# Window attention with a routed feed-forward: the score product in two 64x64 tiles instead of four 32x32, with some TensorE and VectorE work moved behind the product

## What is computed

```
xs = roll(layernorm_c(x)) for a shift of 0 and of 2        # along channels and rows
for each half of the channels (32) and each shift:
    q, k, v = split(qkv_w @ xs)                            # 1x1 convolution, 8 heads of 4 channels
    lepe = depthwise 3x3 convolution of v
    in each window of 4 x 4 pixels, for each head:
        out = softmax(q k^T * scale + bias) v + lepe       # 16 x 16 scores
x = x + the two shifts' outputs
t = x as tokens;  g = top-2 gates of softmax(layernorm(t) @ router_w + router_b)
t = t + sum over the two chosen experts of gate * (layernorm(t) @ expert_w + expert_b)
```

## Time and profile before

| | us |
|---|---|
| median of 3 runs | 3418.93 (3413.72 to 3419.05) |
| the profiled execution, its own time | 3416.38 |
| its span, first to last instruction | 3414.6 |
| TensorE busy | 3076.2 (90%) |
| GpSimd busy (issuing DMAs) | 2509.8 (74%) |
| VectorE busy | 2233.1 (65%) |
| ScalarE busy | 1619.7 (47%) |

### The profile page before, as it was taken

One profiled execution on the slowest core, in us unless ns is written; L12 is line 12 of the kernel. 1 busy time (PEld: TensorE's weight loads), 2 busy tenths in 40 slices (PEclk: granted clock), 3 DMA queues, 4 the chain that ended last, 5 costly groups with the idle time before them and its releaser, 6 DMA issues.

```text
span 3414.6 us, 201082 instructions
## 1 busy us (share of the span) xinstructions
PE 3076.2 (90%) x84772; PEld 1798.8 (53%) x84772; DVE 2233.1 (65%) x4807; ACT 1619.7 (47%) x3362; POOL 2509.8 (74%) x4998
## 2 busy tenths in 40 slices
PE   4899999989989899998999989999899999999987
PEld 2555555545555455554555545555455555555553
DVE  2566767656666666666666757666666666666666
ACT  2554545445444454444444445444454444444441
POOL 4887777767777677777777767777677777777771
PEclk7999999999999999999999999999999999999998
DMA  2456665656565565556565656666565656565656
GB/s 64 105 138 160 159 160 155 160 131 168 148 167 149 145 165 147 155 153 153 150 168 147 163 139 158 161 155 166 133 170 148 168 152 163 152 162 146 163 138 178
DMA packets 436964, 517.64 MB, mean 152 GB/s; under 512 B 116400, under 2 KB 405168, under 8 KB 435888
## 3 DMA queue, kind: packets, MB, share of 16 engines
q1 hardware_dynamic: 270128, 390.67, 42.8%
q0 software_dynamic: 165888, 113.57, 13.9%
HBM read 312.67 MB, written 77.86 MB: 114 GB/s over the span
## 4 chain that ended last, share of the span: by engine, by line
PE 81%; issue 8%; DVE 5%; ACT 4%; DMA 1%; DVEq 0%; POOL 0%; SPq 0%; ACTq 0%; POOLq 0%
PE bank L632 18%; PE bank L717 14%; PE bank L697 13%; PE bank L617 9%; PE bank L723 4%; PE bank L657 3%; PE bank L670 3%; PE bank L737 3%; PE bank L742 2%; PE bank L731 2%; PE bank L756 2%; PE bank L648 2%; PE bank L748 2%; ACT qx L820 2%; ACT bank L812 1%
## 5 line engine op out<-in xcount | busy, mean ns | idle before, releaser
L585 POOL DMA_DIRECT2D vx<-vt x3072 | 1562.1, 517 | 443.6 <-PE bank L723 433.8
L573 POOL DMA_DIRECT2D kx<-k_sb x1536 | 739.2, 489 | 386.7 <-issue 241.7
L717 PEld LDWEIGHTS bank<-probT,vx 128*32 128x32 f32 x36864 | 605.5, 150 | 445.9 <-issue 387.8
L717 PE MATMUL bank<-probT,vx 128*32 128x16 f32 x36864 | 668.0, 210 | 146.9 <-issue 132.7
L632 PEld LDWEIGHTS bank<-kx,qx 32*32 32x32 f32 x36864 | 598.1, 112 | 345.4 <-issue 332.4
L632 PE MATMUL bank<-kx,qx 32*32 32x64 f32 x36864 | 700.7, 226 | 76.6 <-issue 54.2
L949 DVE TENSOR_TENSOR gx<-gate_wide,yn_pair 128x768 f32<-128x768 f32 x384 | 365.6, 953 | 384.5 <-PE bank L617 380.4
L697 PE MATMUL bank<-halo,conv_w 128*64 128x380 f32 (+6 forms) x2592 | 479.5, 497 | 0.1
L806 ACT ACTIVATE prob<-prob 128x512 f32<-128x512 f32 x576 | 360.0, 625 | 244.4 <-DVE prob L961 222.3
L961 DVE TENSOR_TENSOR prob<-bank,row_max 128x512 f32<-128x512 f32 x576 | 398.5, 692 | 16.7
L956 DVE TENSOR_REDUCE row_max<-bank 128x32 f32<-128x512 f32 x576 | 382.8, 665 | 37.8 <-PE bank L632 33.2
(11 more groups left out here) (72 smaller groups left out, 2959.9 us busy)
## 6 DMA issues: line engine op xcount, KB each, us to landing
gate_wide<-gate_rows SPq DMA_DIRECT2D x768, 192.0 KB, 3.9
vx<-vt POOLq DMA_DIRECT2D x3072, 12.0 KB
halo<-xn SPq DMA_DIRECT2D x160, 240.0 KB
kx<-k_sb POOLq DMA_DIRECT2D x1536, 24.0 KB
z<-fin SPq DMA_DIRECT2D x192, 192.0 KB
yn_pair<-yn POOLq DMA_DIRECT2D x384, 96.0 KB, 3.2
xa<-in_x SPq DMA_DIRECT2D x96, 192.0 KB, 3.1
xn<-xa SPq DMA_DIRECT2D x192, 96.0 KB, 2.5
```

The lines of the kernel that those rows point to most:

```text
L573: pool.dma_start(kx[to + m:to + C:4, r % 2, m, :], k_sb[at + m:at + C:4, r % 2, :])\
L585: pool.dma_start(vx[to:to + TOK, r % 2, col:col + 25:8, odd, :], vt[at:at + TOK, r % 2, x::2, :, :].rearrange("p h n k -> p h (n k)"))\
L717: last = MM(bank_o[32 * c:32 * c + 32, at * TOK:(at + 1) * TOK], vx[:, kr % 2, :, at % 2, at // 2 * 4 + ba], probT[:, kr % 2, at, ba * TOK ...
```

## The change

It has five parts.

1. The score's matmuls: two per window, 64 rows and 64 weight columns each, in place of four of 32 and 32; the streamed columns stay 64. For that `qx` has four masked copies of q in place of two, so `mask_q` has four columns and ScalarE makes four copies a strip (`Q_PARTS`).
2. ScalarE copies k out of its bank ahead of the copies of q.
3. Convolution sides 1 and 2 stand behind the product of their slot (side 0 stays ahead of it).
4. The expert products with place 1 stand behind the product: number 2 in slot 1, and number 3 in slot 2, which had place 0 before.
5. VectorE's `tile_out` stands at the end of its slot, behind `turn_p`.

```diff
-EXPERT_AT = {(0, 0): 0, (1, 0): 1, (1, 1): 2, (2, 0): 3}
+EXPERT_AT = {(0, 0): 0, (1, 0): 1, (1, 1): 2, (2, 1): 3}
...
-        "mask_q": ((p[:, None] // 16 & 1) == np.arange(2)[None, :]) * HD ** -0.5,
+        "mask_q": ((p[:, None] // 16 & 3) == np.arange(4)[None, :]) * HD ** -0.5,
...
-        qx = sb("qx", [128, 2, WIN, 2, TOK])
+        qx = sb("qx", [128, 2, WIN, 4, TOK])
...
                     for w in range(UW):
                         win = j * UW + w
-                        for g in range(4):
-                            at = slice(g * CH, g * CH + CH)
+                        for half in range(2):
+                            at = slice(half * C, half * C + C)
                             last = MM(bank_s[r % 2][at, w * KEYS:(w + 1) * KEYS],
                                       qx[at, kr % 2, win, :, :].rearrange("p a i -> p (a i)"),
                                       kx[at, kr % 2, :, win * TOK:(win + 1) * TOK],
...
-                expert(1)
                 if ti := s.tile("logits"):
...
-                if (ti := s.in_tile("conv")) and ti[2] < len(SIDES):
+                conv((0,))
                 if u := s.unit("product"):
...
+                expert(1)
+                conv((1, 2))
                 if ti := s.tile("centre"):
...
-                        pe.wait_ge(q_saved, (2 * k - 3) * 2)
+                        pe.wait_ge(q_saved, (2 * k - 3) * Q_PARTS)
...
                 if st := s.strip("query_key"):
+
+                    k, r = st
+                    act.wait_ge(k_made, k + 1)
+                    if s.later(r, 2):
+                        act.wait_ge(k_spread[r % 2], k // 2 * (K_DMAS * 16))
+                    S.activation(by_window(k_sb[:, r % 2, :]), windows(bank_p[1][:, 0:SPX]),
+                                 ACT.Copy).then_inc(k_saved, 1)
+                if st := s.strip("query_key"):
                     k, r = st
...
-                    for a in range(2):
+                    for a in range(Q_PARTS):
```

More of the change, by code:

```diff
@@ L401, in metaformer_block @@
         N_SPREAD_CLEARED = 2
-        XS_DMAS, K_DMAS, V_DMAS, GATE_DMAS = 5, 8, 16, 2
+        Q_PARTS, XS_DMAS, K_DMAS, V_DMAS, GATE_DMAS = 4, 5, 8, 16, 2
         block = ctx.enter_context(nc.Block())
@@ L619, in expert, with conv @@
                     last.then_inc(expert_made, 1)
+                def conv(sides):
+                    ti = s.in_tile("conv")
+                    if not ti or ti[2] not in sides:
+                        return
+                    k, r, side = ti
+                    t, dw = (r + 1) % IMT, SIDES[side]
+                    if side == 0:
+                        pe.wait_ge(halo_loaded[r % 2], halos_to(s, r) * 16)
+                        if s.later(r, 1):
+                            pe.wait_ge(y_step, k * 2 - 1)
+                    low, high = max(0, -dw), W - max(0, dw)
+                    first = [side == 0, side == 0]
+                    for group, skip in ((0, 0), (1, 2)):
+                        parts = [(half, *rows) for half in range(2) for rows in conv_rows(t, half)[group]]
+                        for half, top, end, which in sorted(parts, key=lambda part: part[1]):
+                            at = half * SP + skip
+                            last = MM(by_rows(bank_c[half * C:(half + 1) * C, 0:SPX])[:, top:end, low:high],
+                                      conv_w[:, which, group * 3 + side, :],
+                                      by_rows(halo[:, r % 2, :])[:, at + top:at + end, low + dw:high + dw],
+                                      start=first[half], stop=(side == 2 and group == 1), skip_group_check=True)
+                            first[half] = False
+                    if side == 2:
+                        last.then_inc(conv_made, 1)
                 if u := s.unit("score"):
@@ L625, in slot @@
                         pe.wait_ge(k_spread[kr % 2], (k // 2 + 1) * (K_DMAS * 16))
-                        pe.wait_ge(q_saved, (k + 1) * 2)
+                        pe.wait_ge(q_saved, (k + 1) * Q_PARTS)
                     wait_alone(pe, bias_placed, n + 1)
@@ L740, in slot @@
                     pe.wait_ge(fsq_made, k + 1)
-                    pe.wait_ge(q_saved, strips_to(s, 2 * k + 10) * 2)
+                    pe.wait_ge(q_saved, strips_to(s, 2 * k + 10) * Q_PARTS)
                     MM(bank_p[0][:, 0:SPX], const("mean"), ysq[:, :], start=True, stop=True).then_inc(fvar_made, 1)
@@ L815, in slot @@
                     k, r = st
-                    if s.later(r, 2):
-                        act.wait_ge(score_made, (k - 1) * UNITS)
-                    act.wait_ge(q_made, k + 1)
-                    for a in range(2):
[L820 to L825, removed]
                     act.wait_ge(k_made, k + 1)
@@ L830, in slot @@
                                  ACT.Copy).then_inc(k_saved, 1)
+                if st := s.strip("query_key"):
+                    k, r = st
+                    if s.later(r, 2):
+                        act.wait_ge(score_made, (k - 1) * UNITS)
+                    act.wait_ge(q_made, k + 1)
+                    for a in range(Q_PARTS):
+                        S.activation(qx[:, r % 2, :, a, :].rearrange("p n (r w) -> p n r w", w=SP),
+                                     windows(bank_p[0][:, 0:SPX]), ACT.Copy,
+                                     scale=const("mask_q")[:, a:a + 1]).then_inc(q_saved, 1)
                 if ti := s.tile("centre"):
@@ L964, in slot @@
                 gate_product(0)
[L965 to L970, removed]
                 if st := s.strip("divide"):
@@ L1026, in slot @@
                 gate_work((10, 12), (0, 0))
+                if yt := s.tile("tile_out"):
+                    k, r = yt
+                    dve.wait_ge(expert_made, (k + 1) * PAIRS)
+                    if s.later(r, 2):
+                        dve.wait_ge(out_stored[r % 2], k // 2 * 16)
+                    V.tensor_tensor(y_out[:, r % 2, :], bank_f[:, 0:SPX], y[:, r % 4, :], ALU.add).then_inc(y_out_made, 1)
             pipeline(dve, slot)
```

## The result

The changed kernel takes 3158.43 (median of 4 runs, 3155.91 to 3167.26), against 3416.32 (4 runs, 3407.16 to 3419.05) for the kernel before beside it: a ratio of 0.9261, interval 0.9237 to 0.9286. I had forecast 3190. The profiled execution has a span of 3165.4.

A forecast was written before the change was run, and what follows sets the result against it. TensorE was taken as the bound, losing time to idling, instruction fetch and a lowered clock. The terms gave 31.5 a tile against 34.1, so 2.6 over 87 tiles, 226, and 3190; range 3120 to 3290 for 8 in 10.

The forecast's parts named there:

- The bound, and "issue" as instruction fetch: TensorE, busy 3076.2 of 3414.6, bounds the kernel; its "issue" waits (132.7 product, 54.2 score) are waits for instruction packets.
- what stays of the fetch: TensorE's instruction fetch after the change: stalls of 0.1 to 0.8 at some packet boundaries, taken as 0.2 a tile.
- The score, +0.03 a unit: Score matmuls on TensorE: 64-column loads stay hidden except the first of a unit; +0.03 a unit, 0.18 a tile.
- the rival with exposed loads: Score on TensorE: 64-column loads not hidden, a unit takes 1.82, +0.8; 3650 in all, chance 0.1.
- Fetch and chain cover each other: Slot 3 before `tile_sum`: fetch stalls and the chain to k's copy overlap, so removing one alone would give little.
- `tile_sum` at 3.4: Slot 3: k's copy 0.93 and row maximum 0.4 earlier, so `tile_sum` starts at 3.4, not 4.75; 1.35 a tile.
- The stall in slot 4, 0.43: TensorE in slot 4: a stall whose removal was to take 0.43 off the tile of 32.74.
- Convolution behind the product, "taken as 0": Convolution and experts behind the product: same instructions, cost taken as 0; up to 1.4 in slots 0 and 5 without cover.
- `centre` +0.2: Slot 0: `centre` waits 0.2 a tile for ScalarE's four copies of q, which now follow k.
- The 0.3 a tile for a clock that still falls: TensorE's clock: 0.3 added to the tile's 31.2 for a clock falling now and then, making 31.5.
- the rival "the fetch stays": TensorE's fetch: stalls covered by the chain show in full, 1.2 to 1.6 a tile plus 1 clock; 3355, chance 0.12.
- The sum: Whole tile: 32.74 less 1.35 and 0.43, plus 0.2, 0.18 and 0.2, written as 31.2; with 0.3 for the clock, 31.5.

The follow-up runs named there:

- The order alone: Changed kernel with the score back in four 32x32 tiles and two copies of q, its order on all engines kept: 3338.99, ratio 0.9775 to the kernel before.
- `tile_out` early: Changed kernel with expert products 2 and 3 ahead of the product again and `tile_out` back early on VectorE: 3215.14, ratio 0.9392 to the kernel before.

## Why the prediction was right

**The bound, and "issue" as instruction fetch: right.** Undoing the larger tiles, and with them the lower number of instructions, brought 182 of "issue" back with breaks inside groups; putting the tiles alone into the kernel before took them away (52). The times at which the packets landed say the same. For what stays of the fetch I had 0.2 a tile: outside the loop's five returns 12 of the 35.3 are left, 0.14 a tile.

**The score, +0.03 a unit: right in kind, small in size.** It is 1.08 where it was 1.02 to 1.03, so +0.05, 29 in all instead of 17. The 64-column loads stay hidden, and the rival with exposed loads (1.8 a unit) is out. The loads in the earlier trace rows differ in columns alone, so that rows don't count is not in them; a list of all loads has 189 ns for 48 rows by 128 columns and 192 to 224 ns for 128 by 128.

**Fetch and chain cover each other: right, and stronger than said.** I wrote that removing one alone "would give little". The order alone gives 2.2%, k's place alone 1.0%, and the tiles alone cost 2.1%, because their two extra copies of q stand ahead of k.

**`tile_sum` at 3.4: 0.3 too early.** The step "together I put the row maximum at 0.4 into slot 3" failed; it is at 0.68. `tile_out` and the transpose before it fill VectorE without a gap.

**Slot 2: missed.** It takes 4.04 where it took 4.42, and no term of my sum has these 0.38. In the kernel before its product and the next score waited behind `fin` and the bias, which VectorE's idle 1.36 delayed; with `tile_out` early the slot is 4.47 again. The two misses, 0.3 and 0.38, nearly cancel.

**The stall in slot 4, 0.43: too small.** 0.43 is the idle time in the row. From start to start that score took 1718.39 - 1716.65 = 1.74 (1718.39 is the start of the convolution behind it), where 1.03 is usual, so the stall cost 0.71; the slot fell from 6.60 to 5.93.

**Convolution behind the product, "taken as 0": wrong.** It costs 0.26 in slot 5, about 25 in all.

**`centre` +0.2: right**, 24.8 over 93 times; q first in slot 0 removes it.

**The clock: right in level, with the 0.3 too cautious.** The forecast asked for 0.97 or more and it is 0.980. The 0.3 a tile for a clock that still falls were not needed: at none of 88 `tile_sum` did it fall. One could put the lowered clock down to the long wait for k alone, since with 182 of "issue" and short waits for k it is 0.977, and with 24 to 52 of "issue" and 2.6 of waiting for k it is 0.934 and 0.926. The kernel before with k ahead of q speaks against that: hardly a wait for k, and 0.956. What orders the kernels is how long TensorE stands still in slot 3 before `tile_sum`, whatever it waits for (median idle time of a tile, and tiles in which the clock fell there, all between 200 and 3000):

| | idle | clock fell |
|---|---|---|
| changed kernel | 0.70 | 0 of 88 |
| the order alone | 0.77 | 6 of 83 |
| k ahead of q on the kernel before | 1.39 | 35 of 82 |
| kernel before | 1.82 | 58 of 81 |
| changed kernel, q ahead of k | 2.59 | 77 of 80 |
| larger tiles alone | 2.68 | 76 of 79 |

So the rival "the fetch stays", which let the clock fall behind the fetch's breaks, was right that they can do it. With the new order and the old tiles few did: of the 182 there 60 stand in slot 3 before `tile_sum`, of the 187 in the kernel before 101.

**The sum was added up wrongly, and the slip helped.** The terms give 32.74 - 1.35 - 0.43 + 0.2 + 0.18 + 0.2 = 31.54, not the 31.2 that I wrote; with them the tile is 31.84, the gain 34.1 - 31.84 = 2.26 a tile or 197, and the forecast about 3220. That lies in the range as well, but 3190 is nearer to the measured 3158 by luck. The same slip is in the rival of the fetch, whose 3355 would be about 3385. A tile fell by 1.43 (32.74 to 31.31), where the terms, rightly added, said 1.20. With the score's 0.05 taken out of each slot, slot 2 gave 0.43 and slot 4 0.29 more than the terms had, and the 0.2 for the fetch didn't show in this tile; on the other side slot 3 gave 0.25 less, slot 5 cost 0.25, the score 0.12 and slots 0 and 1 together 0.07 more than the terms had. Over the whole loop the mean turn fell from 418.2 to 384.2, 2.84 a tile, which for 87 tiles is 247 and matches the measured 249; the forecast had 2.6. The mechanism was right; the sum came close in part because its misses cancel.

## What to carry to other kernels

When an engine breaks off inside a group of identical instructions that wait for nothing, count the instructions between the breaks and compare with the packets of the instruction queue: if they agree, the number of instructions is a resource of its own, and larger tiles can save time even where the stream is as long as before. When two limits end the same slot, each experiment on one of them alone will mislead; here the parts gave +2.1% and -2.2%, and together -7.4%. Look at what else the engine's standing still costs, the clock above all: a small shift of one wait can move much more than its own length. And before adding copies to an engine, look at what stands behind them in its order: the same four copies of q are nearly free behind k (24.8 of waiting at `centre`) and cost 8% ahead of it.

## What the runs showed of the hardware

- A gap ahead of `tile_sum` of 0.43 (changed kernel) or 0.80 (`tile_out` early) left the clock where it was; after one of 2.59 (q ahead of k) or 2.68 (larger tiles alone) the groups behind it ran at 1.2 GHz, the score in 1.97 instead of 1.15. In the kernel before, at 1749.64, the same came after a break of 1.53 by the fetch and 0.55 of waiting for k.
- Every one of the 130 breaks called "issue" in the kernel before (over 0.25) ended 1.20 to 1.82 after a packet of the instruction queue had landed.
- 32 pairs of load and matmul with one column, on four tiles of the array in turn, took 0.36, 0.011 each.
- The order of two groups that don't depend on each other changes their time: `value`, product, convolution, `router` 4.11, with the convolution ahead 3.85.
- Each of the loop's returns still costs one long fetch (4.3 to 5.4 in the changed kernel).
